# Flamingo block with gated cross attention and a mixture of experts: the last 64 rows of the down products contracted as 128

## The reference

```python
def _expert(h, g, u, d):
    return jnp.einsum('...i,hi->...h', jax.nn.silu(h @ g.T) * (h @ u.T), d)
shared_out = _expert(x, sg, su, sd)
probs = jax.nn.softmax(x @ wr.T + rb, axis=-1)
scores, idx = jax.lax.top_k(probs, 2)          # then normed to sum 1
w = jnp.sum(scores[..., None] * jax.nn.one_hot(idx, 7), axis=-2)
out = shared_out
for e in range(7):
    out = out + w[..., e:e + 1] * _expert(x, rg[e], ru[e], rd[e])
```

## Time and profile before

| | |
|---|---|
| median of three runs | 1322.37 us |
| profiled execution | 1324.38 us |
| its span | 1322.6 us |
| mean granted TensorE clock over it | 0.994 |
| PE busy | 1288.4 us, 97% of the span |
| DVE, ACT, POOL busy | 896.4, 847.9, 386.1 us |

### The profile page before, as it was taken

How to read it: one execution, slowest core, us unless ns; L and a number is a source line. 1 busy time by engine, 2 the same in 40 slices (tenths; PEclk the granted TensorE clock), 3 DMA queues, 4 the chain that set the end, 5 groups by cost and what they waited for, 6 DMA issues and landing times.

```text
span 1322.6 us, 23635 instructions
## 1 busy us (share of the span) xinstructions
PE 1288.4 (97%) x7916; PEld 687.9 (52%) x7917; DVE 896.4 (68%) x1787; ACT 847.9 (64%) x1203; POOL 386.1 (29%) x625
## 2 busy tenths in 40 slices
PE   7999999999999999999999999899999999999996
PEld 4654333333333333333333333445558888888885
DVE  6788899999999999999999997456322222222221
ACT  4654888888888888888888887531113444444441
POOL 5566122242232422422323223210001333333331
PEclk9999999999999999999999999999999999999999
DMA  7774222433423324334233243274031111211221
GB/s 245 234 239 160 80 76 83 130 98 92 130 82 108 115 83 126 100 87 138 83 110 116 83 125 123 74 277 207 1 116 40 32 32 32 32 32 32 32 33 23
DMA packets 87094, 133.55 MB, mean 101 GB/s; under 512 B 20459, under 2 KB 55019, under 8 KB 85978
## 3 DMA queue, kind: packets, MB, share of 16 engines
q1 hardware_dynamic: 78394, 122.15, 30.0%
q0 software_dynamic: 7296, 9.97, 4.7%
q10 hardware_dynamic: 1312, 0.27, 0.1%
HBM read 84.36 MB, written 47.55 MB: 100 GB/s over the span
## 4 chain that ended last, share of the span: by engine, by line
PE 88%; DVE 2%; DMA 2%; issue 1%; SPq 1%; POOL 1%; ACT 0%; POOLq 0%; DVEq 0%; ACTq 0%
PE ps L792 18%; PE ps L947 15%; PE ps L772 13%; PE ps L671 13%; PE ps L977 8%; PE ps L903 6%; PE ps L914 4%; PE ps L775 3%; PE ps L683 2%; PE ps L679 2%; PE ps L746 1%; PE ps L675 1%; DMA o_parts<-work 1%; DMA arena<-rowst 1%; PE ps L941 1%
## 5 line engine op out<-in xcount | busy, mean ns | idle before, releaser
L1452 DVE TENSOR_REDUCE mx<-ps 128x1 f32<-128x512 f32 (+3 forms) x960 | 594.0, 652 | 45.5 <-PE ps L671 18.4
L1131 ACT ACTIVATE arena<-ps 128x1024 f32<-128x1024 f32 (+1 forms) x512 | 480.5, 989 | 66.8 <-PE ps L772 58.9
L792 PE MATMUL ps<-arena 128*32 128x512 f32 (+3 forms) x2048 | 273.2, 567 | 2.2 <-POOL arena L1350 1.7
L1350 POOL TENSOR_SCALAR_AFFINE_SELECT arena<-arena 128x128 f32<-128x128 f32 x256 | 75.1, 293 | 491.7 <-ACT arena L1131 485.4
L772 PE MATMUL ps<-arena 98*128 98x512 bf16 x624 | 197.8, 380 | 1.7 <-DMA arena<-rowst 1.6
L947 PE MATMUL ps<-work,arena 128*128 128x128 f32 x1672 | 196.8, 277 | 1.4 <-DVE work L1756 1.4
L671 PE MATMUL ps<-arena 96*128 96x512 bf16 x576 | 197.1, 381 | 0.6 <-DVE mx L1452 0.6
L947 PEld LDWEIGHTS ps<-work,arena 128*128 128x128 f32 x1672 | 189.5, 192 | 13.9 <-issue 12.3
L1399 POOL DMA_INDIRECT out<-bv,slot_table x38 | 59.9, 1575 | 203.2 <-DVE bv L1772 195.2
L1223 ACT ACTIVATE work<-ps 128x512 f32<-128x512 f32 x38 | 22.7, 597 | 147.5 <-PE ps L947 147.5
L977 PE MATMUL ps<-arena,work 128*128 x456 | 112.2, 388 | 0.9 <-DVE bv L1772 0.9
(11 more groups left out here) (182 smaller groups left out, 1537.0 us busy)
## 6 DMA issues: line engine op xcount, KB each, us to landing
arena<-in_experts SPq DMA_DIRECT2D x8, 2176.0 KB, 16.1
o_parts<-work SPq DMA_DIRECT2D x63, 256.0 KB, 3.1
arena<-k_parts SPq DMA_DIRECT2D x48, 198.1 KB, 3.1
arena<-k_parts SPq DMA_DIRECT2D x48, 132.1 KB, 2.8
k_parts<-work SPq DMA_DIRECT2D x16, 300.0 KB, 3.7
q_parts<-work SPq DMA_DIRECT2D x12, 384.0 KB, 3.0
arena<-q_parts SPq DMA_DIRECT2D x48, 96.0 KB, 2.2
work<-recip_rows SPq DMA_DIRECT2D x16, 256.0 KB
```

The costliest lines, as they stand in the source:

```text
L792: mm = pe.matmul(ps[32 * q:32 * q + VW, 6, first:T], vst[:, r % VR, TT + kt if cross else kt, :], pr[:, c0:c0 + T - first], start=(phase = ...
L1131: act.activation(pr[:, c0:c0 + n], ps[:, 2 * (g % 2):2 * (g % 2) + 2, :].rearrange("p b n -> p (b n)")[:, 0:n], ACT.Exp, scale=SCALE).then ...
L1350: pool.affine_select(out=exps, in_=exps, pattern=[[1, P]], compare_op=ALU.is_ge, fill=0.0, base=0, channel_multiplier=-1).then_inc(S["mask ...
L1452: return dve.tensor_reduce(m, out, AX_X, ALU.max)
```

## The change

The sixth slice of both down products is contracted over all 128 partitions. The down weights have zeros there already; the other operand gets them:

- Shared experts: `hT[0]` and `hT[1]` get zeros in partitions 64 to 127 of the sixth slice by one POOL memset each. The first stands behind POOL's last attention work; the second also waits until the normed rows that lay there are stored (`first_rows`) and turned (`xn_turned`). Silu and product write only partitions 0 to 63 of that slice, so the zeros stay. PE waits for them (`rest_zeros`) before the first two down products.
- Routed experts: `hidT` now holds five slices for each of its two buffers, and the sixth lies in `hid_rest`, 2 x 128 columns at the place of the sixth slice of `hT[0]`, whose zeros it inherits. Since slices 4 and 5 are no longer side by side, ACT's second Silu becomes two instructions.

```diff
--- before.py
+++ after.py
@@ -332,7 +332,8 @@
         xg = wp
         yt = bv
         xgT = work[:, 0:4 * P].rearrange("p (b k t) -> p b k t", b=2, k=2)
-        hidT = work[:, 4 * P:4 * P + 2 * IT * P].rearrange("p (b i t) -> p b i t", b=2, i=IT)
+        hidT = work[:, 4 * P:4 * P + 2 * WHOLE * P].rearrange("p (b i t) -> p b i t", b=2, i=WHOLE)
+        hid_rest = work[:, WHOLE * T:WHOLE * T + 2 * P].rearrange("p (b t) -> p b t", b=2)
 
 
         gu_of = weights[:, :, 0:4 * I].rearrange("p e (j k i) -> p e j k i", j=2, k=2)
@@ -345,7 +346,7 @@
                  "m_all m_hi m_split rows_tr rows_evac rows_ready masked o_evac o_even o_odd rest_evac rest_even rest_odd parts_free den_in num_in den_half den_sum den_third num_half num_third num_sum recip_done recip_out recip_in y_cross y_self y_done dve_chain "
                  "pool_chain proj_mm xn_turned xn_freed x2_ready tanh_done bias_gated x_biased wr_ready logits_mm logits_out logits_turned gap_ready exp2_done "
                  "first_rows rows_out took_ready counts_mm counts_out lane_ready table_mm table_out "
-                 "shared_load routed_load route_load up_mm silu_done h_done down_mm acc_done gathered0 gathered1 turned xT_ready "
+                 "shared_load routed_load route_load up_mm silu_done h_done rest_zeros down_mm acc_done gathered0 gathered1 turned xT_ready "
                  "copied up2_mm silu2_done h2_done down2_mm y_ready scattered based routed").split()
         S = {n: sem(n) for n in names}
         scr = [S[f"scr{i}"] for i in range(NS)]
@@ -907,11 +908,13 @@
             def shared_down(tb, t0=0, t1=TT):
                 if tb and t0 == 0:
                     pe.wait_ge(S["acc_done"], tb)
+                if tb < 2 and t0 == 0:
+                    pe.wait_ge(S["rest_zeros"], tb + 1)
                 pe.wait_ge(S["h_done"], (tb + 1) * IT)
                 for t in range(t0, t1):
                     out = ps[:, 4 + t // 2, (t % 2) * C:(t % 2 + 1) * C]
-                    for it, (i0, m) in enumerate(SHARED_CUTS):
-                        mm = pe.matmul(out, hT[tb % 2][0:m, it, t * P:(t + 1) * P], wds[0:m, it, :],
+                    for it in range(IT):
+                        mm = pe.matmul(out, hT[tb % 2][:, it, t * P:(t + 1) * P], wds[:, it, :],
                                        start=(it == 0), stop=(it == IT - 1))
                 if t1 == TT:
                     mm.then_inc(S["down_mm"], 1)
@@ -972,9 +975,9 @@
                     if not (isinstance(i, int) and i == 0):
                         pe.wait_ge(S["y_ready"], i)
                 for it in range(half * IT // 2, (half + 1) * IT // 2):
-                    m = CUTS[it][1]
                     o = 4 * I + it * C
-                    mm = pe.matmul(ps[:, 4, 0:C], hidT[0:m, b, it, :], weights[0:m, bass.ds(e, 1), o:o + C],
+                    h = hidT[:, b, it, :] if it < WHOLE else hid_rest[:, b, :]
+                    mm = pe.matmul(ps[:, 4, 0:C], h, weights[:, bass.ds(e, 1), o:o + C],
                                    start=(it == 0), stop=(it == IT - 1))
                 if half:
                     mm.then_inc(S["down2_mm"], 1)
@@ -1226,8 +1229,8 @@
                     act.wait_ge(S["up2_mm"], i * 3 + 2)
                     copy_main(e, 1)
                 act.wait_ge(S["up2_mm"], i * 3 + 3)
-                act.activation(hidT[:, b, HALF:IT, :].rearrange("p i t -> p (i t)"), ps[:, 2, 0:2 * P], ACT.Silu
-                               ).then_inc(S["silu2_done"], 1)
+                act.activation(hidT[:, b, HALF, :], ps[:, 2, 0:P], ACT.Silu)
+                act.activation(hid_rest[0:REST, b, :], ps[0:REST, 2, P:2 * P], ACT.Silu).then_inc(S["silu2_done"], 1)
                 if ahead:
                     copy_last(e)
 
@@ -1381,6 +1384,11 @@
             num_sums(NGRP - 1)
             outputs(NGRP - 1)
 
+
+            pool.memset(hT[0][REST:P, WHOLE, :], 0.0).then_inc(S["rest_zeros"], 1)
+            pool.wait_ge(S["first_rows"], 16 * (HT_TILES // TT))
+            pool.wait_ge(S["xn_turned"], 2 * (HT_TILES // TT))
+            pool.memset(hT[1][REST:P, WHOLE, :], 0.0).then_inc(S["rest_zeros"], 1)
 
 
             def gather(i):
@@ -1762,7 +1770,7 @@
                 first = hidT[:, b, 0:4, :].rearrange("p i t -> p (i t)")
                 dve.tensor_tensor(first, first, ps[:, 1, :], ALU.mult).then_inc(S["h2_done"], 1)
                 dve.wait_ge(S["silu2_done"], i * 2 + 2)
-                dve.tensor_tensor(hidT[0:REST, b, WHOLE, :], hidT[0:REST, b, WHOLE, :], ps[REST:P, 2, P:2 * P], ALU.mult)
+                dve.tensor_tensor(hid_rest[0:REST, b, :], hid_rest[0:REST, b, :], ps[REST:P, 2, P:2 * P], ALU.mult)
                 dve.tensor_tensor(hidT[:, b, 4, :], hidT[:, b, 4, :], ps[:, 2, 2 * P:3 * P], ALU.mult).then_inc(S["h2_done"], 1)
 
             def result(i, b, first):
```

## The result

The changed kernel takes 1303.05 us (median of four runs, 1302.31 to 1303.45) where the kernel before takes 1322.89 (four runs, 1322.32 to 1327.22): a ratio of 0.984, 95% interval 0.982 to 0.986. A later set of runs gave 1303.28 against 1323.41, 0.986 (0.984 to 0.988). 1302.2 was forecast, on a median before of 1322.37; with the fourth run before, which makes it 1322.89, the same 20.2 us would give 1302.7. The profiled execution took 1303.45 against 1324.38, its span 1301.7 against 1322.6.

The account below looks back on a forecast made before the run. PE (TensorE) was taken to bound the kernel. 6.2 - 0.1 + 14.2 - 0.1 = 20.2 us off the median of 1322.37 gave 1302.2 us, own range 1300.5 to 1304, chance 0.86.

Parts of the forecast that it names:

- The price: Both down products: each pair of 64-row matmuls costs PE an excess of 0.385 us over 128-row pitch.
- The mechanism: PE's 64-row pairs: changing the tiling mode drains TensorE, leaving the load engine idle 0.33 us on both sides.
- what it was called for: Projection's 0.223 us pitch, ends of accumulations included, to show the price isn't that of ending an accumulation.
- The shared part: Shared down products: 16 pairs at 0.385 give 6.2 us off PE, less 0.1 charged.
- (a): Next up product's third group waits for DVE's product on the first hidden slice; just fits, 0.1 us charged.
- (b): Third block's accumulation, awaited by PE before the fourth block, moves with PE's end of the third; cost none.
- the 37th slot: 37th routed down product: DVE scales its result before PE goes on, so half the excess counts, 0.2 us.
- the better of the two cases: Last expert's weights: if their load follows the routing, ACT's copies start at 986.1, otherwise at 989.2.
- The routed part: 38 routed down products: 14.2 us gained, 13.9 of it from the first 36, less 0.1 in the first turn.
- the last product: 38th routed down product: little of its 0.3 us is seen, bounds 0 and 0.3, 0.1 taken as gain.
- ACT's split: ACT's second Silu as two instructions: DVE's operand 0.12 us later, covered except in the first routed turn, 0.1 once.
- cover of 1.06 us: Routed turns: time left between DVE's copy of the next turned rows and PE's next load, from 1.18 before.

Follow-up runs that it names:

- the delayed Silu: Changed kernel with ACT's last three weight copies and three idle copies ahead of the second Silu in each routed turn; 1331.09 us, ratio 1.007.

## Why the prediction was right

The time fell inside the forecast's own range and for the reason given. The hit is nearer than the terms deserve, for some of their errors cancel.

- **The price.** 0.385 us a pair was forecast. The turns give 8.113 - 7.722 = 0.391 (the new turn from 1139.01 back to the down product at 1007.74: 131.27 / 17), the shared blocks 0.395. The pitch was read as 0.2165 and is 2.59 / 12 = 0.2158.
- **The mechanism.** The runs show that the price is that of going from whole-array rows to 64 or fewer and back: none at 65 and 96 rows, the same at 64 and 32, the same in the third and the sixth place, none inside a stretch, one price for a stretch of two or four matmuls. The Trainium skill's sentence that changing the tiling mode drains TensorE ("TensorEngine Tiling (Array Packing)", "Key Properties") agrees with all five. That the array runs empty is not seen itself, and stays a reading. What the trace of the kernel before has is this, the pair's matmuls behind the load at 1154.47 of the earlier trace rows:
```profile
1154.48 0.70 PE L977 MATMUL ps<-arena,work 64*128 x2
```
The pair's first load starts 0.30 us behind the last 128-row matmul (1154.17), where a matmul follows the other in 0.2165, and its matmul starts 0.01 behind it: the load no longer runs ahead of the matmul that it serves. An array that must be empty first would do this, and so would a load that may not pass a matmul of another form for another reason; no run tells these apart, and the price is the same. The Trainium skill's other rule, that a load goes by columns and not by rows, is true of the load (0.29 us for two of 64 rows, 0.30 for two of 128) and tells nothing of this price.
- **A misreading.** The projection of the earlier trace rows has four accumulations of two products, so of four records, and not eight of two records. Its pitch of 0.223 us still holds three ends of accumulations, so what it was called for stands.
- **The shared part.** 6.1 us was forecast from the first shared down product to the first routed one, where it is 5.92, and 6.03 with the interval behind. Sixteen stretches at 0.395 would be 6.3. Charge (a), 0.1 us for DVE's product, wasn't paid: the row below has it end at 922.17 + 0.69 = 922.86, 16.65 us behind PE's first down product where 16.75 had been worked out, and PE's load came in step. What was missed is in (b), the start of the fourth block, put at nothing. The third and the fourth block's down products, before and after:
```profile
976.49 11.94 PE L914 MATMUL ps<-arena,work 128*128 128x256 f32 x48
990.18 6.03 PE L914 MATMUL ps<-arena,shared 128*128 128x256 f32 x24 [1.75 <-DVE x L1675]
...
972.77 10.57 PE L917 MATMUL ps<-arena,work 128*128 128x256 f32 x48
985.10 5.45 PE L917 MATMUL ps<-arena,shared 128*128 128x256 f32 x24 [1.75 <-DVE x L1683]
```
From the one to the other it is 13.69 us before and 12.33 after, 1.36 less where four pairs are 1.58. PE waits here for DVE either way, so the way out of the block's last pair was no cost, as the prediction has it for the 37th slot.

DVE behind the first shared down product, and ACT's first weight copy, after the change:
```profile
922.17 0.69 DVE L1586 TENSOR_TENSOR work<-work,ps 128x512 f32<-128x512 f32 x1
...
984.54 2.00 ACT L1212 ACTIVATE arena<-arena 128x1024 f32 x2 [11.27 <-DMA arena<-in_experts]
```
- **The cover of the expert weights.** The copy from the last weights started 4.66 us earlier than in the earlier trace rows, 0.58 of which is the earlier start of the stage. It follows the routing, as the better of the two cases had it; POOL's first gather, which follows it too, moved by 3.14 us on the same count, as the 3.1 of the forecast, and why the weights came 0.9 sooner still isn't known. The copies end at 987.46 and PE's first routed product stands at 995.78.
- **The routed part.** 14.1 us forecast, 14.24 measured. Of its terms the 36 turns gave 36 x 0.391 = 14.1 instead of 13.9, the 37th product 0.19 (3.62 us to the last one for 3.81) as worked out, the first turn's longer wait took 0.05, and the last product gave nothing where 0.1 was counted as gained: the last scatter-add waits for the landing of the one before, in both kernels.
- **ACT's split.** 0.12 us of delay was charged, once. The rows of a turn show two instructions of 0.28 and 0.26 us that overlap, and DVE's copy:
```profile
1131.27 0.28 ACT L1232 ACTIVATE work<-ps 128x128 f32<-128x128 f32 x1 [0.19 <-PE ps L950]
1131.44 0.26 ACT L1233 ACTIVATE work<-ps 64x128 f32<-64x128 f32 x1
...
1132.24 0.42 DVE L1764 COPY work<-ps 128x256 f32<-128x256 f32 x1
```
The second ends 0.43 us after the first starts, where one Silu took 0.38: 0.05 us. But the cover of 1.06 us that the prediction set against it was too large by the 0.23 us from DVE's end to PE's start, which it didn't count (the up product waits for three semaphores one after another; the fourth shared block's load, with DVE's last, starts 0.05 us behind it, 985.09 for 983.38 + 1.66 = 985.04). It made no difference here; the delayed Silu shows what it would have made.
- **The zeros.** POOL's two memsets took 0.52 and 0.53 us, ready at 866.63 and 884.22, and no PE row waits for them.
- **The sum.** 20.2 us was forecast; the medians give 19.8 and the spans 20.9, of which 0.6 lies ahead of the changed stages; PE's stretch gives 20.27. A price read 0.006 to 0.01 us a pair too small (0.4 us in all) and the 0.1 charged in (a) stand against the 0.2 missed in (b) and the 0.1 counted at the end. That they largely cancel is luck; each is small, and none touches the mechanism.

## What to carry to other kernels

A tail of 64 or fewer contracted rows (64 and 32 were tried) in the middle of 128-row products isn't free: here, in float32 with 128 loaded and 256 streamed columns and at 2.4 GHz, each stretch of them cost about 0.39 us of TensorE, with nothing in a table of waits to show it but "issue" on the loads. Where TensorE is the bound and operands can hold zeros (or one row more), contract 65 or more rows; where they can't, put the short slices of neighbouring accumulations side by side. Other data types and shapes were not tried. And when a stretch of cover is weighed, take the release off it: from the end of DVE's instruction to the start of TensorE's load it was 0.23 us with three waits in a row here, and 0.05 at the fourth shared block.

## What was not expected

The same program ahead of the changed stages takes different times from run to run: the first shared down product stood at 906.79, 906.21, 904.36, 905.03, 903.92, 905.83, 904.19, 907.09, 904.07, 905.54 and 905.93 us in the eleven profiles, 3.2 us from the least to the most, while from there to the first routed product the kernels with the same shared part agree to 0.01 us (89.57 in five profiles, 89.62 with 96 rows). What is uncertain of this kernel's time lies in the attention part, so a difference of a microsecond behind it is read from its stage and not from the medians. The clock doesn't account for it: ahead of that product the stretches at 1.2 GHz add up to 6.8 us both in the profile with 903.92 and in the one with 907.09. Which step of the attention part varies isn't known.
